# Layer 0 of a two-layer image kernel: another order of work between images and inside a row's matmuls

## What is computed

```python
def _gn(v, G=8, eps=1e-5):        # group norm: mean and variance over 2 channels and all pixels
    ...
    return ((g - m) / jnp.sqrt(s + eps)).reshape(v.shape)
def _L0_conv_ref(x, w_real, w_imag, b_real, b_imag):
    X = jnp.fft.rfftn(x, axes=(-2, -1), norm='backward')
    Xr, Xi = (jnp.real(X), jnp.imag(X))
    ...                           # 3x3 complex convolution over the half spectrum, 16 -> 16 channels
    return jnp.fft.irfftn(Y, axes=(-2, -1), norm='backward')
def _L1_conv_ref(x):              # mean filter 15 x 15
    ...
x = x + _L0_conv_ref(_gn(x), L0_conv_w_real, ...)
x = x + _L1_conv_ref(_gn(x))
```

## Time and profile before

| | |
|---|---|
| time, median of 3 runs | 4111.79 us (4107.49 to 4116.27) |
| profiled execution, its own time | 4116.43 us |
| span from first to last instruction | 4114.6 us |
| mean granted TensorE clock | 0.957 of full speed |
| busy: PE, DVE, ACT, POOL | 90%, 77%, 64%, 64% of the span |

### The profile page before, as it was taken

The page is one execution under the profiler, slowest core; times in us unless marked ns, Lnnn a source line. Parts: engine busy times, 40 slices in busy tenths (PEclk is TensorE's granted clock), DMA queues, the critical chain, the costliest instruction groups (busy, mean ns, idle before and its releaser), DMA issues.

```text
span 4114.6 us, 122879 instructions
## 1 busy us (share of the span) xinstructions
PE 3688.1 (90%) x41056; PEld 2642.1 (64%) x41056; DVE 3153.9 (77%) x5926; ACT 2618.7 (64%) x4792; POOL 2634.6 (64%) x2177
## 2 busy tenths in 40 slices
PE   3299998998989989899898998899988998989988
PEld 1166676666766667566675666666676666766667
DVE  7778877787867878678786887778877787777876
ACT  0089833997249962599527993289833997349962
POOL 5078852887538865488546885378852887538865
PEclk8599999999999999899999999999999999999999
DMA  7411165111741128211381114711165111741114
GB/s 164 160 43 51 40 186 157 50 51 36 226 124 49 51 58 241 84 51 51 94 240 49 51 51 133 208 41 51 43 179 164 50 51 32 223 128 52 51 48 137
DMA packets 228435, 406.74 MB, mean 99 GB/s; under 512 B 98160, under 2 KB 173520, under 8 KB 215888
## 3 DMA queue, kind: packets, MB, share of 16 engines
q1 hardware_dynamic: 205776, 285.88, 24.2%
q10 hardware_dynamic: 22400, 117.46, 10.5%
HBM read 256.31 MB, written 146.80 MB: 98 GB/s over the span
## 4 chain that ended last, share of the span: by engine, by line
PE 70%; DVE 10%; POOL 9%; issue 6%; ACT 2%; DMA 1%; ACTq 1%; SPq 1%; DVEq 0%; POOLq 0%
PE p L554 21%; PE h_ps L622 14%; PE h_ps L445 13%; PE p L648 6%; PE p L483 4%; PE xt_ps L435 4%; POOL ob_all L1252 3%; POOL arena L1245 2%; PE h_ps L554 2%; PE p L598 2%; POOL ob_all L1254 2%; DVE ob_all L1177 2%; POOL arena L1268 2%; ACT arena L697 1%; DMA img<-in_x 1%
## 5 line engine op out<-in xcount | busy, mean ns | idle before, releaser
L554 PE MATMUL p<-arena,bd_all 64*64 64x512 f16 x16896 | 1220.2, 380 | 17.2 <-DVE ob_all L1109 8.8
L1245 POOL TENSOR_TENSOR arena<-arena 128x512 f16<-128x512 f32 x512 | 593.7, 1159 | 607.1 <-ACT arena L727 580.5
L554 PEld LDWEIGHTS p<-arena,bd_all 64*64 64x64 f16 x16896 | 613.8, 105 | 383.7 <-issue 188.5
L697 ACT ACTIVATE arena<-h_ps 128x512 f16<-128x512 f32 x512 | 305.7, 597 | 835.1 <-PE h_ps L622 594.7
L1303 POOL TENSOR_TENSOR arena<-img 128x512 f32<-128x512 f32 x392 | 498.7, 1273 | 467.4 <-PE h_ps L622 438.6
L445 PE MATMUL h_ps<-hilbert,arena 128*128 128x256 f16 x6144 | 763.4, 275 | 25.5 <-DVE arena L1082 16.6
L1254 POOL TENSOR_TENSOR ob_all<-ob_all,img 128x512 f32<-128x512 f32 x512 | 662.5, 1294 | 82.9 <-POOL ob_all L1252 72.9
L445 PEld LDWEIGHTS h_ps<-hilbert,arena 128*128 128x128 f16 x6144 | 603.1, 98 | 148.4 <-issue 18.7
L1252 POOL TENSOR_TENSOR ob_all<-ob_all 128x512 f32<-128x512 f32 x512 | 653.7, 1277 | 26.4 <-DVE ob_all L1115 26.4
L1082 DVE SCALAR_TENSOR_TENSOR arena<-h_ps,arena 128x512 f16<-128x512 f32 x512 | 354.1, 692 | 390.3 <-ACT arena L741 389.4
L733 ACT ACTIVATE arena<-xt_ps 128x1024 f16<-128x1024 f16 x512 | 517.4, 1011 | 37.3 <-PE xt_ps L435 37.3
(11 more groups left out here) (164 smaller groups left out, 4537.4 us busy)
## 6 DMA issues: line engine op xcount, KB each, us to landing
out<-ob_all SPq DMA_DIRECT2D x512, 256.0 KB, 4.4
bd_all<-bd_dram SPq DMA_DIRECT2D x512, 192.0 KB, 2.3
img<-in_x ACTq DMA_DIRECT2D x168, 512.0 KB, 7.1
img<-in_x ACTq DMA_DIRECT2D x112, 256.0 KB, 4.9
wrap_mat<-tab_wrap_h SPq DMA_DIRECT2D x512, 32.0 KB, 2.0
img<-in_x SPq DMA_DIRECT2D x24, 512.0 KB, 24.5
bd_dram<-ob_all SPq DMA_DIRECT2D x16, 768.0 KB, 3.5
img<-in_x SPq DMA_DIRECT2D x16, 256.0 KB, 6.8
```

Source lines behind the costliest of these rows:

```text
L554: m = mm(bank[out_half * HP:(out_half + 1) * HP, :], low(half, 6 * lm + (j if own else j + 1)), (g_part if own else h_part)(half, lp), sta ...
L1245: G.tensor_tensor(gp[s][:, 1, :], g32, gp[s][:, 0, :], ALU.subtract).then_inc(g_split, 1)
```

## The change

Seven things, in six loops of instructions:

1. **mix**: the lower half now starts on `p0`, the upper half on `p1`, so that both work from the first step; the boundary row is added by quarters of the array as well (`wrap_terms`), as a tenth step of each half. Waits: `x1_done` moves to the start, `t2_done` from step 1 to step 3 of the upper half, `v_wrap` (first row only) to step 3 of the lower half.
2. **ACT's correction column** goes to DVE (`half_mean`, one instruction for both columns, placed before `low_hilbert`); `add_half_row` comes one row later (n-4).
3. **Statistics**: the chain is two links shorter, and for an input five instructions less stand ahead of `s_scale`. PE does `group_mean` and `group_variance` between the steps of the virtual Hilbert matmul (`input_statistics`), not behind them.
4. **Image loop**: `virtual_input` stands behind ACT's jump; the DVE work on the virtual rows up to `vz_split` ahead of DVE's jump.
5. **First rows**: PE does the products of the virtual rows first and L512 behind the first turn; `c_tab` is in a bank of `h_ps`. The means of the virtual rows (L1076, L1077, L529) and the work on `known` go behind the first and the second row. ACT has `normalise(0, 3)` and `wrap_high` ahead of its row loop.
6. **SP** holds the stores of the last two pairs of an image until the last load of the next has landed.
7. **POOL** sums row t-5 instead of t-4, and its row loop starts at t = 16 instead of 12.

The core of the diff:

```diff
+        c_tab = h_ps[:, 1, 0:3 * P].rearrange("p (i t a) -> p i t a", i=3, a=2)
...
                 for j in range(T // 2):
+                    if j == T // 2 - 2:
+                        sp.wait_ge(loaded_pair[LAG // 2 - 1], b * 32 + 64)
+                        sp.sem_inc(stores_held, 1)
                     store(b, j, j % NS)
...
+            def input_statistics(b):
                 pe.wait_ge(uv_kept, b + 1)
                 for k in range(4):
                     m = mm(uvT_ps[:, k, :], uv32[:, k * P:(k + 1) * P], tb["ident"][:], start=True, stop=True)
                 m.then_inc(vxt_made, 1)
+                group_mean(b * 2 + 1)
                 pe.wait_ge(vxt_kept, b + 1)
                 for a in range(2):
+                    if a == 1:
+                        group_variance(b * 2 + 1)
...
+                virtual_scales(b)
...
+                    def lower(r):
+                        if r < 3:
+                            half_terms(p0[s], 0, r, 0, True, False)
+                        elif r == 3:
...
+                            wrap_terms(0, False).then_inc(p0_half, 1)
+                        elif r < 7:
                             if r == 4:
                                 pe.wait_ge(p1_half, n + 1)
                                 pe.sem_inc(mix_step, 1)
+                            m = half_terms(p1[:], 2, r - 4, 0, False, True)
...
+                        else:
                             if r == 7:
+                                pe.wait_ge(p2_half, n + 1)
+                                pe.sem_inc(mix_step, 1)
+                            m = half_terms(p2[:], 4, r - 7, 0, False, True)
...
+                    def upper(r):
+                        if r < 3:
+                            m = half_terms(p1[:], 2, r, 1, True, False)
+                            if r == 2:
+                                m.then_inc(p1_half, 1)
+                        elif r < 6:
+                            if r == 3:
+                                pe.wait_ge(t2_done, PRIMED + n)
+                                pe.sem_inc(mix_step, 1)
+                            m = half_terms(p2[:], 4, r - 3, 1, True, False)
+                            if r == 5:
+                                m.then_inc(p2_half, 1)
+                        elif r < 9:
+                            if r == 6:
                                 pe.wait_ge(p0_half, n + 1)
                                 pe.sem_inc(mix_step, 1)
+                            half_terms(p0[s], 0, r - 6, 1, False, False)
+                        else:
+                            wrap_terms(1, True).then_inc(p0_ready, 1)
+                    for r in range(10):
+                        for part in ((upper, lower) if r in (4, 7) else (lower, upper)):
+                            part(r)
...
             def image(b, follow):
+                virtual_input(b)
                 deviation(b * 2 + 1)
...
+                def half_mean(n, t, s, first):
+                    if first * NG + s >= NG:
+                        dve.wait_ge(x1_whole, n - NG + 1)
+                    dve.wait_ge(x1_counted, n + 1)
+                    V.scalar_tensor_tensor(half_row[:, s, :], stat[:, t, 1:6:3], -0.5, known[:, t, :],
+                                           ALU.mult, ALU.add).then_inc(half_made, 1)
...
+                slot(0, 0, 0)
+                virtual_means()
+                slot(0, 1, 0)
+                known_means()
```

More of the change, by code:

```diff
@@ L508, in vm @@
                     return vmat[:, j, :]
[L509 to L513, removed]
                 pe.wait_ge(vg_split, b + 1)
@@ L520, in layer0 @@
                 edge_terms(vm, NV).then_inc(v_mixed, 1)
-                pe.wait_ge(c_kept, b + 1)
                 front_turn(b * T, 0)
+                pe.wait_ge(kappa_made, b + 1)
+                for i in range(3):
+                    for f in range(3):
+                        m = mm(c_tab[:, i], block_mat[:, 3 * i + f, :], kappa[:, f], start=(f == 0), stop=(f == 2))
+                m.then_inc(c_made, 1)
                 front_hilbert(b * T)
@@ L561, in mix, with wrap_terms @@
                     pe.wait_ge(t1_done, PRIMED + n)
+                    if first > 0:
+                        pe.wait_ge(x1_done, PRIMED + n - (NG - 1))
                     pe.sem_inc(mix_step, 1)
[L563 to L574, removed]
-                                pe.sem_inc(mix_step, 1)
[L576 to L584, removed]
+                    def wrap_terms(half, closes):
+                        for out_half in (half, 1 - half):
+                            m = mm(p0[s][out_half * HP:(out_half + 1) * HP, :],
+                                   wrap_mat[s][half * HP:(half + 1) * HP, out_half * HP:(out_half + 1) * HP],
+                                   wrap_row[half * HP:(half + 1) * HP, :], start=False, stop=closes,
+                                   skip_group_check=True)
+                        return m
+                    def lower(r):
+                        if r < 3:
+                            half_terms(p0[s], 0, r, 0, True, False)
+                        elif r == 3:
+                            if first == 0 and s == 0:
+                                pe.wait_ge(v_wrap, b + 1)
+                                pe.sem_inc(mix_step, 1)
+                            wrap_terms(0, False).then_inc(p0_half, 1)
+                        elif r < 7:
                             if r == 4:
@@ L603, in layer0 @@
                     front(0, s, 0)
+                    if s == 1:
+                        pe.wait_ge(c_kept, b + 1)
+                        pe.wait_ge(v_means, b + 1)
+                        for j in range(3):
+                            m = mm(c_ps[:, 40 + 2 * j:42 + 2 * j], tb["from_virtual"][:, j, :], vmean[:],
+                                   start=True, stop=True)
+                        m.then_inc(v_meant, 1)
                     if s == NG - 1:
@@ L744, in add_half_row @@
                 def add_half_row(n, t, s):
-                    act.wait_ge(x1_counted, n + 1)
-                    for a in range(2):
-                        ins = nc.scalar.activation(half_row[:, s, a:a + 1], stat[:, t, 1 + 3 * a:2 + 3 * a], ACT.Identity,
-                                                   bias=known[:, t, a:a + 1], scale=-0.5)
-                    ins.then_inc(half_made, 1)
                     act.wait_ge(half_made, n + 1)
@@ L805, in image @@
                     slot(T // NG - 1, s, T // NG - 1)
-                for t in range(T - 3, T):
+                for t in range(T - 4, T):
                     add_half_row(b * T + t, t, t % NG)
@@ L1284, in layer0 @@
                     split_g(b * T + t, t)
-                for t in range(R + 5):
-                    slot(t // NG, t % NG, t // NG, sum_t=t - 4 if t >= 4 else None)
-                assert (R + 5) % NG == 0
-                with pool.Fori((R + 5) // NG, T // NG - 1) as i:
+                for t in range(R + 9):
+                    slot(t // NG, t % NG, t // NG, sum_t=t - 5 if 5 <= t <= R + 5 else None)
+                assert (R + 9) % NG == 0
+                with pool.Fori((R + 9) // NG, T // NG - 1) as i:
                     for s in range(NG):
@@ L1291, in layer0 @@
                 for t in range(T - NG, T):
-                    slot(t // NG, t % NG, t // NG, sum_t=t - 4 if t - 4 >= T - R else None)
+                    slot(t // NG, t % NG, t // NG, sum_t=t - 5 if t - 5 >= T - R else None)
                 add_terms(b * T + T - 1, T - 1, (T - 1) % NG, T // NG)
-                for t in range(T - 4, T):
+                for t in range(T - 5, T):
                     presum(b * T + t, t)
```

140 lines of the change are left out of this document (67 added, 73 removed).

## The result

After takes 4040.26 us, median of 4 runs (4036.1 to 4042.02), against 4110.07 for the kernel before: ratio 0.9827, interval 0.981 to 0.9844. I had forecast 3980. The range held it, but it lies where rival 2 put it (4042). The profiled execution took 4036.1, span 4034.3: 80.3 less than the one profiled before.

What follows compares the result with a forecast made beforehand. PE was taken to bound layer 0's rows, and a chain of waits the time between images. Rows 62 plus between images 70 made 132 us off the median of 4111.8: 3980, range 3908 to 4046.

Steps and rivals of the forecast that it cites:

- rival 2: Layer 0 rows: the waits eat the whole 0.34 us, only the chain between images gains 70; 4042 us, chance 0.14.
- rows: Layer 0: the row period falls from 4.48 to 4.34 us, 7.8 per image, 62 us in all.
- change of layers: Between layers: two links of 0.19 us and ACT's column leave the chain; 0.5 per image, 4 us in all.
- second wait: PE's mix, lower half at r = 7, two steps behind its cause: another 0.06 to 0.11 us late per row.
- first wait: PE's mix, lower half at r = 4, two steps behind the upper half's step: 0.08 to 0.12 us late.
- the 0.34 that I called ideal: PE's mix: the next Hilbert matmul at 1308.97 instead of 1309.31, 0.34 us earlier per row if nothing were lost.
- Rival 1: PE's mix: halves don't hold each other up, 0.24 or 0.34 us saved per row; 3935 or 3890 us, chance 0.21.
- Are the others able to follow?: Layer 0 rows at 4.34 us: ACT needs 3.90, DVE about 4.0, POOL 3.84, so all fit.
- small instruction: DVE's row in layer 0: the new instruction takes 0.16 us, at most 0.3, where DVE waits for ACT.
- Rows with POOL's sums: Layer 0: seven rows per image stay at POOL's 5.11 us, costing 7 x 0.14 = 1.0 us more per image.
- Between images: Chain between images: stores held, jumps hidden, products in the low clock; gains 70 us in all, bounds 45 and 85.
- Rival 3: Jumps between images: idle time isn't from the jumps and stays, chain gains 38 instead of 70; 4012 us, chance 0.10.

Runs made afterwards that it cites:

- Experiments 3: Changed kernel with the upper half's matmuls issued first in steps 4 to 8, not in 4 and 7 alone: 3985.19 us, ratio 0.9692.
- experiment 4: Changed kernel with the upper half issued first in step 5 too (4, 5 and 7), nowhere else: 3985.83 us, ratio 0.9692.
- experiment 2: Kernel before with the new mix alone, ACT keeping its column: 4068.24 us, ratio 0.9891.
- experiment 10: Kernel of experiment 3 with POOL waiting until known is corrected and until the tail's correction and the mean are made: 3968.0 us, ratio 0.9652.
- experiment 11: Kernel of experiment 10 with the correction column on ACT again, as two ACTIVATEs: 3983.71 us, ratio 0.969.
- Experiments 5: Changed kernel with an image's last stores issued at once, SP's wait for the last load taken out: 4049.17 us, ratio 0.9843.
- experiment 7: Changed kernel with ACT's virtual_input ahead of its jump, as before: 4056.62 us, ratio 0.9862.
- experiment 6: Changed kernel with the correction column back on ACT, half_mean taken out: 4028.61 us, ratio 0.9797.

## Why the prediction was half right

The forecast was 62 + 70 = 132 us. By the profiled executions it was 80.3, and the stretches of the two traces, summed over all eight images, add up to it:

| term | forecast | measured | from |
|---|---|---|---|
| rows | 62 | 7 x 3.65 - 0.4 = 25 | fifth row's Hilbert matmul to the last row's |
| starts of images | 6 x 8.8 + 7 + 6 = 66 | 6 x 8.9 + 5.8 + 4.1 = 63 | filter's first matmul to the fifth row's Hilbert matmul |
| change of layers | 8 x 0.5 = 4 | -7 x 1.07 - 0.7 = -8 | last row's Hilbert matmul to the filter's first matmul |
| sum | 132 | 80 | 80.3 measured |

The -0.4 is the last image, whose long rows eat what the shorter period gives.

**The row: the mechanism of the second wait was wrong.** I wrote that "the upper half's step 5 stands behind the lower half's in the queue, falls as far behind, and the second wait is again two steps from its cause: another 0.06 to 0.11". The upper half isn't held back: its step 5 starts on time at 831.81, the next ones at 832.03, 832.25 and 832.51, and it finishes ahead of the lower half. What comes in order is the count that a matmul gives. So `p2_half` was bound to the *late lower* step issued in front of it, and the weight loads stood still 0.32, not 0.18. Experiments 3 and 4 show it: another order of issue in one step takes 0.14 off the row. That is all that the second wait cost, since in experiment 4 the lower half's step 7 isn't late at all, and I had put it at 0.06 to 0.11. The first wait makes the lower half 0.12 late in both kernels (forecast 0.08 to 0.12). Of the 0.34 that I called ideal, the kernel after kept 0.06; I had let it keep 0.11 to 0.20. The number of rival 2 (4042) was met, but not its condition: 0.28 of the 0.34 was lost, not all, and the time from a matmul to the one that waits for it is not "0.6": only the second looks so long, because of the count. That the time fell on rival 2's is luck: it has the rows at 0 and the rest at 70, and they gave 25 and 55. Rival 1 had the halves' independence right and its price wrong, since it left out the count.

Which of a matmul's two ends comes in order, the Trainium skill (TensorE: Matmul & The Clock Gate, The mechanism) doesn't split: it has both strictly in program order. The counts here agree; the starts don't, since in step 9 the lower half is issued first and starts at 832.92, the upper at 832.75. The page on TensorEngine Tiling (of the Trainium skill, Key Properties), by which tiles run independently, fits the starts.

**Are the others able to follow?** Yes, but for the last image: experiment 2 rules ACT out at 4.42, and at 4.28 no engine but PE is full in the first seven images. In the last one DVE is busy 96% (95% in experiment 10), by the small instruction that I had put at 0.16. I had ACT at 3.90 without the column; with it I'd have put 4.50, and experiment 11 shows 4.35; probably much of the column's wait on itself is covered when ACT is pressed, which no run took apart.

**Rows with POOL's sums.** I charged 1.0 per image because POOL's 5.11 stays. After, they cost 1.7 over 4.42 each image as before over 4.48, so the shorter row didn't cost there; at 4.28 they cost 3.0 over it (five rows of 4.7 to 5.0), and there the charge applies.

**Between images: right** (though for the last and the first image I had put 7 and 6, and 5.8 and 4.1 came). ACT's table load starts before the sums end and is done 0.2 after them; PE no longer stands at a jump behind the group norm; the sums run without a gap; the products take 5.64 us in place of 3.89 because they now catch the low clock (granted 0.50, the lower level, from 1167.85 to 1170.40, in their first half; forecast 5.9), and L527 2.23 (forecast 2.1). Experiments 5 and 7 give 9 us to the held stores and 16 to ACT's place. Two links were not in my sum: the second row's gap is gone, as forecast, but the third now waits 0.64 for DVE; and PE waits 0.57 for ACT's `virtual_base` (L783) and DVE behind it ahead of L532.

**The cost of the small instruction: wrong twice.** I took 0.16, "at most 0.3", from links that ran with POOL idle, and put it "where DVE waits for ACT". In the middle of layer 0 that holds in seven images (0.15), and in the last it takes 0.91. At the end of layer 0 it stands in the chain, beside POOL's sums, at 1.23 for two, and pushes L1198 to 1.42. And moving the work on `known` behind the second row put it beside POOL's additions: L1122 has 2.85 us for four, 1.00 before.

**Rival 3** (idle time at jumps stays) fell with experiment 7. What is left open: the 12 us of experiment 6, of which the trace shows 8, while the profiled spans differ by 1.7; what moves L1163 beside POOL's work in the last image; the difference of the 80.3 of one pair of profiled executions to the 69.8 of the medians; and the worth of the new order of products and L512, which no run took apart. Undoing that part alone wasn't tried.

## What to carry to other kernels

When one matmul waits for another's count, what matters isn't only the distance to that matmul but what was issued just in front of it: put the matmul that others wait for ahead of one that is itself late. A small VectorE instruction is to be priced by where it stands: two inputs in on-chip memory and GpSimd at work beside it cost up to one whole GpSimd instruction (L1228, with one tile and two scalar columns as its inputs, was stretched too), in a loop even in every row once the two have slipped into step, so either shift GpSimd's work behind the chain by a wait or keep such links off DVE there. And a load taken off an engine that isn't the bound earns nothing until the bound has moved: here it cost 8 us by the trace and 12 by the medians first, and was worth 16 after 0.14 had been taken off PE's row.

## What the runs showed of the hardware

- From a 512-column matmul's start to the weight load that waits for its semaphore there were 0.50 to 0.51 us, and 0.65 where a matmul issued ahead of it had started 0.14 later. Counts came in the order of issue in these rows, though matmuls on the other rows of the array started out of order (832.75 ahead of 832.92).
- DVE instructions stretched from 283 to 1236 ns (L1122), 0.55 to 1.52 us (L1228), 0.33 to 1.42 us (L1198), 0.22 to 1.27 us (L999), 0.15 to 1.15 us (L1163 in the last image) while a POOL TENSOR_TENSOR of 1.16 to 1.35 us ran, and ended 0.01 to 0.28 us behind its end. L1156, which reads one input, takes 0.69 to 0.70 us in all 512 rows.
- Where it jumps back over an image's instructions ACT was idle for 4.36 and 4.47 us and DVE for 3.02; behind an engine that waits anyway it cost nothing.
